# Cross-attention and routed layer on one core: first weights on ScalarE's queue, a warming of eleven products, first values loaded later

## The reference, cut to what matters

```python
# x, ctx: (8, 128, 512); 32 heads of width 128; position_bias (32, 128, 128)
h   = rmsnorm(layernorm(x)) * ln_weight
q   = h @ w_q.T;  k = ctx @ w_k.T;  v = ctx @ w_v.T          # w_q, w_k, w_v: (4096, 512)
s   = softmax(where(mask, q @ k^T + position_bias, -inf))    # per tile and head
x   = x + layernorm(x) + (s @ v) @ w_out.T
n   = layernorm(x)
r   = softmax(n @ gate_w.T)                                  # 8 experts
out = x + ((n * (r @ in_channel_scale)) @ sign(weight).T) * (r @ out_channel_scale) + bias
```

## Time and profile before

| | us |
|---|---|
| median of 3 runs | 844.12 |
| lowest and highest | 843.89, 844.49 |
| the profiled execution | 844.16 |
| its span, first to last instruction | 842.4 |
| PE busy | 833.7 (99%) |
| DVE busy | 619.5 (74%) |
| ACT busy | 392.1 (47%) |
| POOL busy | 301.4 (36%) |

### The profile page before, as it was taken

One profiled execution on the slowest core, in us unless ns is written; L12 is line 12 of the kernel. 1 busy time (PEld: TensorE's weight loads), 2 busy tenths in 40 slices (PEclk: granted clock), 3 DMA queues, 4 the chain that ended last, 5 costly groups with the idle time before them and its releaser, 6 DMA issues.

```text
span 842.4 us, 12886 instructions
## 1 busy us (share of the span) xinstructions
PE 833.7 (99%) x4356; PEld 699.5 (83%) x4356; DVE 619.5 (74%) x1005; ACT 392.1 (47%) x1009; POOL 301.4 (36%) x279
## 2 busy tenths in 40 slices
PE   9999999999999999999999999999999999999998
PEld 8878888888888878788888888888888888888886
DVE  5777856778766795877777777777777877777765
ACT  5632522432441444545544555554554455466673
POOL 2013211022030043625435444544544554535145
PEclk9999999999999999999999999999999999999999
DMA  8355463573452748423144124314413421423002
GB/s 274 138 180 184 150 237 125 168 273 117 146 192 100 224 166 267 165 100 117 51 150 154 65 96 154 102 58 157 137 50 127 153 99 63 153 92 131 1 1 101
DMA packets 60720, 114.07 MB, mean 135 GB/s; under 512 B 5208, under 2 KB 38872, under 8 KB 55408
## 3 DMA queue, kind: packets, MB, share of 16 engines
q1 hardware_dynamic: 60656, 113.25, 39.3%
HBM read 77.58 MB, written 35.65 MB: 134 GB/s over the span
## 4 chain that ended last, share of the span: by engine, by line
PE 90%; DVE 6%; issue 1%; ACT 1%; DMA 1%; POOL 1%; DVEq 0%; POOLq 0%; ACTq 0%; SPq 0%
PE out L1334 10%; PE out L1336 10%; PE out L1335 10%; PE proj L1334 9%; PE proj L1336 9%; PE proj L1335 9%; PE o L1425 6%; PE s L1406 6%; PE s L1334 3%; PE s L1335 3%; PE s L1336 3%; PE t L1414 3%; PE proj L1501 1%; PE s L1382 1%; DMA w_stage<-in_wq 1%
## 5 line engine op out<-in xcount | busy, mean ns | idle before, releaser
L926 ACT ACTIVATE probs<-probs,neg_max 128x128 f32<-128x128 f32 x256 | 99.7, 391 | 135.6 <-DVE neg_max L1179 135.6
L757 POOL TENSOR_TENSOR w_stage<-w_stage 128x256 f32<-128x256 f32 x30 | 25.2, 841 | 308.9 <-DMA w_stage<-in_wk 148.0
L769 POOL TENSOR_TENSOR w_lo<-w_stage,w_hi 128x512 fp32r<-128x512 f32 (+1 forms) x52 | 59.2, 1148 | 147.0 <-ACT w_hi L864 147.0
L1334 PE MATMUL out<-wo_hi,o_hi 128*128 128x512 f32 x224 | 95.3, 426 | 0.2 <-DVE acc L1208 0.2
L1211 DVE TENSOR_TENSOR acc<-out,acc 128x512 f32<-128x512 f32 x100 | 68.4, 688 | 35.7 <-PE out L1336 35.2
L1334 PE MATMUL proj<-x_hi,w_hi 128*128 128x512 f32 x210 | 88.5, 422 | 0.2 <-DVE ring L1038 0.2
L1336 PE MATMUL out<-wo_lo,o_hi 128*128 128x512 f32 x224 | 88.2, 394 | 0.0
L1335 PE MATMUL out<-wo_hi,o_lo 128*128 128x512 f32 x224 | 87.5, 391 | 0.0
L1336 PE MATMUL proj<-x_lo,w_hi 128*128 128x512 f32 x210 | 82.7, 394 | 0.0
L1335 PE MATMUL proj<-x_hi,w_lo 128*128 128x512 f32 x210 | 82.0, 391 | 0.0
L781 POOL TENSOR_TENSOR bias_mask<-bias_raw,mask_neg 128x512 f32<-128x512 f32 x64 | 75.7, 1194 | 13.3 <-DVE probs L1176 13.2
(11 more groups left out here) (352 smaller groups left out, 2141.9 us busy)
## 6 DMA issues: line engine op xcount, KB each, us to landing
k_spill<-ring SPq DMA_DIRECT2D x64, 256.0 KB, 2.8
v_spill<-ring SPq DMA_DIRECT2D x64, 256.0 KB, 2.2
w_stage<-in_wk SPq DMA_DIRECT2D x32, 256.0 KB, 3.3
big_stage<-in_wv SPq DMA_DIRECT2D x8, 1024.0 KB, 7.7
w_stage<-in_wq SPq DMA_DIRECT2D x32, 256.0 KB, 4.1
k_first<-k_spill SPq DMA_DIRECT2D x8, 1024.0 KB, 6.9
v_first<-v_spill SPq DMA_DIRECT2D x8, 1024.0 KB, 4.8
wo_raw<-in_wo SPq DMA_DIRECT2D x16, 512.0 KB, 3.3
```

What stands on the lines that cost most here:

```text
L769: pool.tensor_tensor(lo, staged(m, part), hi.bitcast(F32), ALU.subtract).then_inc(g_wlo, 1)
L926: last = act.activation(probs[:, j % 2, b, :], probs[:, j % 2, b, :], ACT.Exp, bias=neg_max[:, col:col + 1], accum_out=row_sum[:, col:col ...
L1334: pe.matmul(to[:], left_hi, right_hi, start=first and n == 0, stop=False, skip_group_check=True)
```

## The change

- `WARM_UP` goes from 48 to 11. The warming now multiplies a 128x128 tile of ones (in `ring`) by itself; VectorE writes the ones with a memset as its first instruction. Nothing waits for the warming's end.
- The weights of pair 0 are loaded in four halves of 128 KB (`first_load(i, k)`), of which ScalarE issues three, (0,0), (1,0) and (0,1), as its first instructions, and SP the fourth, (1,1), after the four context loads of token half 0. Each half has its own semaphore, and `plain_weights_high` waits for its half alone. The weights of pair 1 are loaded as before.
- `("XX", 3)` moves from (k+5, 4) to (k+6, 4).
- The step that loaded keys and then values is split in two, KL and VV. KL stands where it stood; the values of pair 0 move one cycle on, to (k+8, 1), behind the loads of the second pair of query weights (`w_q` pair 1, at slot 0 of that cycle). For all other pairs VV follows KL at once.

```diff
-WARM_UP = 48
+WARM_UP = 11
@@ schedule
     put(k + 5, 3, ("XT", "T4"))
-    put(k + 5, 4, ("XX", 3))
     put(k + 5, 6, ("XX", 5))
     put(k + 6, 1, ("XX", 4))
-
-    put(k + 7, 1, ("BL", 0), ("BL", 1), ("KV", 0))
+    put(k + 6, 4, ("XX", 3))
+
+    put(k + 7, 1, ("BL", 0), ("BL", 1), ("KL", 0))
+    put(k + 8, 1, ("VV", 0))
...
-    put(q + 1, 1, ("KV", 1))
+    put(q + 1, 1, ("KL", 1), ("VV", 1))
@@ loads
+        def first_load(i, k):
+
+            to, _, _ = plain_weights(0, i, k)
+            return to, wk[i][:, 2 * k:2 * k + 2].rearrange("p c d -> p (c d)")
@@ sync
-            plain_pair(0, 0)
             context(0, 0)
-            plain_pair(0, 1)
             context(0, 1)
+            to, frm = first_load(1, 1)
+            sp.dma_start(to, frm).then_inc(d_first[1][1], 16)
             context(1, 0)
             context(1, 1)
...
-            def keys_and_values(p):
+            def attention_keys(p):
                 if p >= NPAIR:
                     return
                 saved(group_at["K", p])
-                for t in range(HALF):
-                    saved(group_at["V", p // 4, t])
...
                 sp.dma_start(k_tiles[p % 2][:], k_spill[p]).then_inc(d_k[p % 2], 16)
+
+            def attention_values(p):
+                if p >= NPAIR:
+                    return
+                for t in range(HALF):
+                    saved(group_at["V", p // 4, t])
                 if p >= 2:
                     sp.wait_ge(pe_pv, last_score(p - 2))
                 sp.dma_start(v_tiles[p % 2][:], v_spill[p]).then_inc(d_v[p % 2], 16)
@@ scalar
+            for i, k in ((0, 0), (1, 0), (0, 1)):
+                to, frm = first_load(i, k)
+                act.dma_start(to, frm).then_inc(d_first[i][k], 16)
...
-                act.wait_ge(d_plain[2 * n + i], 16)
+                act.wait_ge(*((d_plain[i], 16) if n else (d_first[i][k], 16)))
@@ vector
+            dve.memset(ring[:, 0, 0, 0:P], 1.0).then_inc(v_ones, 1)
@@ tensor
             def warm_up():
-                pe.wait_ge(g_ident, 1)
+                pe.wait_ge(v_ones, 1)
                 for _ in range(WARM_UP):
-                    last = pe.transpose(s_bank[0][:, 0:P], ident[:], ident[:])
-                last.then_inc(pe_warm, 1)
-                pe.wait_ge(pe_warm, 1)
+                    pe.matmul(s_bank[0][:, 0:P], ring[:, 0, 0, 0:P], ring[:, 0, 0, 0:P], start=True, stop=True)
```

More of the change, by code:

```diff
@@ L269, in schedule @@
             steps += [("S", 4), *prod[7], *prod[3], ("T", 3), ("EXP", 4), ("BM", 5), ("BL", 4), *prod[4],
-                      *outs(0, 0), ("N", 4), ("KV", 2), *sums, ("PV", 3), *outs(0, 1, 2)]
+                      *outs(0, 0), ("N", 4), ("KL", 2), ("VV", 2), *sums, ("PV", 3), *outs(0, 1, 2)]
             continue
@@ L276, in schedule @@
         split_output = [("WO", p + 1)] if 2 * p + 2 == SPLIT else []
-        steps += slot(j + 3, prod[4] + outs(p, 0), outs(p, 1), outs(p, 2), [("KV", p + 2), *sums, *split_output])
+        steps += slot(j + 3, prod[4] + outs(p, 0), outs(p, 1), outs(p, 2), [("KL", p + 2), ("VV", p + 2), *sums, *split_output])
     j = 2 * SPLIT
@@ L436, in xattn_ffn @@
         d_w, d_big, d_ctx = [sem("d_w0"), sem("d_w1")], sem("d_big"), [sem(f"d_ctx{n}") for n in range(8)]
-        d_plain = [sem(f"d_plain{n}") for n in range(2 * PLAIN)]
+        d_plain = [sem(f"d_plain{n}") for n in range(2)]
+        d_first = [[sem(f"d_first{i}{k}") for k in range(2)] for i in range(2)]
         d_save = [sem(f"d_save{n}") for n in range(3)]
@@ L443, in xattn_ffn @@
         d_ffn_w, d_ffn_small, d_out = sem("d_ffn_w"), sem("d_ffn_small"), sem("d_out")
-        pe_warm, pe_prod, pe_x, pe_s, pe_t = [sem(n) for n in ("pe_warm", "pe_prod", "pe_x", "pe_s", "pe_t")]
+        pe_prod, pe_x, pe_s, pe_t = [sem(n) for n in ("pe_prod", "pe_x", "pe_s", "pe_t")]
         pe_pv, pe_out, pe_nt, pe_gate, pe_rt = [sem(n) for n in ("pe_pv", "pe_out", "pe_nt", "pe_gate", "pe_rt")]
@@ L461, in xattn_ffn @@
         v_y, v_ylo, v_prod, v_stats = sem("v_y"), sem("v_ylo"), sem("v_prod"), sem("v_stats")
-        v_last_res, v_n = sem("v_last_res"), sem("v_n")
+        v_last_res, v_n, v_ones = sem("v_last_res"), sem("v_n"), sem("v_ones")
         v_vsum, v_vs4, v_xsum, v_res = sem("v_vsum"), sem("v_vs4"), sem("v_xsum"), sem("v_res")
@@ L631, in plain_pair @@
             def plain_pair(m, row):
-                to = (w_stage[:, 0:3:2], w_stage[:, 5:7], w_stage[:, 1:4:2], w_stage[:, 4:8:3])[2 * m + row]
-                sp.dma_start(to, wk[2 * m + row].rearrange("p (b c) d -> p b (c d)", b=2)).then_inc(d_plain[2 * m + row], 16)
+                to = (w_stage[:, 1:4:2], w_stage[:, 4:8:3])[row]
+                sp.dma_start(to, wk[2 * m + row].rearrange("p (b c) d -> p b (c d)", b=2)).then_inc(d_plain[row], 16)
             def context(half, b):
@@ L736, in last_store @@
                 sp.dma_start(out[B - 1][:, cols], acc[:, B - 1, cols]).then_inc(d_out, 16)
-            walk({"WL": pair_weights, "DL": second_plain_pair, "VL": value_weights, "SAVE": save, "ML": mask_load, "XL": x_load, "KV": keys_and_values,
+            walk({"WL": pair_weights, "DL": second_plain_pair, "VL": value_weights, "SAVE": save, "ML": mask_load, "XL": x_load, "KL": attention_keys, "VV": attention_values,
                   "BL": bias_load, "WOL": output_weights, "AL": residual_load, "SMALL": small_loads, "FW": ffn_weights, "SUM": store, "SUML": last_store})
```

## The result

| | before | after |
|---|---|---|
| median, both timed on one chip | 844.12 (843.87 to 847.37) | 839.60 (838.66 to 839.88) |
| ratio, 95% interval | | 0.9938 (0.9919 to 0.9957) |
| span of the profiled execution | 842.4 | 837.6 |

Five executions of each. The changed kernel is faster: the medians differ by 4.5 us, the ratio says 5.2 us (3.6 to 6.8). Forecast were 3.35.

What follows compares the result with a forecast made beforehand. PE, busy 99% of the span, bounds the kernel, so only its idle or unneeded time can be won. Start 1.4, 303 us 0.55 and 329/338 us 1.4 sum to 3.35: 844.16 to 840.81 us, range 839.2 to 843.0.

Steps and rivals of the forecast that it cites:

- the landings at the start: Start: data land 0.6 us earlier, 0.4 for 128 KB less ahead and 0.2 for issue time; start gains 1.4 in all.
- The bound of 2.8 us: Start: upper bound of the gain, if the dip goes away and the weights are ready at 9.3 us.
- the dip: Start: load rate down to 180 GB/s between 5 and 6 us before the change, which another queue need not cure.
- The hand-over's terms: Keys to queries: 0.65 us at 303, 0 to 0.2 given back; 1.4 at 329 and 338, the first 0.43.
- Start, with unchanged landings: Start, k=1 group: shorter warming alone gains 0.85 us, from 12.16 to the weights' half (0,1) ready at 11.2.
- ScalarE's first piece: Start: ScalarE's first piece, at 3.79 us before; a start after 4.2 us would show the prediction wrong.
- PE's slack: Start: PE's own twelve MATMULs end at 10.0 us, 0.7 us before the k=1 group at 10.75.
- (2): Start: landings stay, as the new queue takes its share ahead of the context; start 0.85 us, 841.4; chance 0.14.
- (5): Start: ScalarE's loads go out late behind its table load, start gains 0; 842.2 to 842.7 us; chance 0.08.
- (3): Read at 338 us: set by ScalarE's table load and exponentials, not the weights; 841.8 us; chance 0.12.
- (1): Start: clock falls or rises late, 512-column MATMULs take 0.46 instead of 0.23 us; 841.8 to 843.3; chance 0.16.
- (4): Start: clock stays low through all eight products of pair 0, 11 us more, 851.8, slower than before; chance 0.05.

Runs made afterwards that it cites:

- x11: The kernel before run once more, unchanged, for a second trace: 842.86 us in one execution.
- x10: The changed kernel run once more, unchanged, against the kernel before: 838.94 us, ratio 0.9936.
- x12: Kernel before with eleven warming products of ones and first weights in whole 256 KB rows from ScalarE's queue, old hand-over: 842.73 us, ratio 0.9988.
- x4: Kernel before with only the hand-over changed (later x_lo sum of part 3, later values of pair 0), start as before: 841.78 us, ratio 0.9974.
- x6: Kernel before with only the values of pair 0 loaded later, behind the second pair of query weights: 842.12 us, ratio 0.9975.
- x2: Kernel before with only the warming changed, to eleven products of ones, all loads as before: 842.87 us, ratio 0.9993.
- x13: The changed kernel with the two altered orders of x9, and POOL's memsets and the small loads moved later: 839.75 us, ratio 0.9949 against the kernel before.
- x3: Kernel before with eleven warming products and the four weight halves, all issued from SP's one queue, old hand-over: 842.06 us, ratio 0.9974.
- x7: The changed kernel with no warming products: 841.57 us, ratio 0.9972 against the kernel before.
- x9: The changed kernel with weights' half (0,1) split before the fourth context piece and another x split two slots later: 838.84 us, ratio 0.9935 against the kernel before.
- x1: Kernel before with only the new loads (four halves, three from ScalarE's queue), old 48 transposes and hand-over: 844.37 us, ratio 1.0012.

## What the prediction had right, and the step that failed

- **The step that failed: the landings at the start.** The prediction gave earlier landings 0.6 us, 0.4 for bytes and 0.2 for the rest, "as the rate dipped to 180 GB/s between 5 and 6 us, which another queue need not cure". The context loads landed 1.5 to 1.6 us earlier (8.90 to 7.27, 9.5 to 8.0; 1.4 between x11 and x10), and the start gave 2.41 us in place of 1.4. Two things in the term were wrong. It counted at most 0.66 us of issue time as saved and took 0.2 of it, but the load that decides was issued 1.37 us sooner (3.49 to 2.12), since the second row of weights was no longer in front of it either and the loads before it were issued faster. And it held the rate fixed: from 5 to 8 us the engines moved 376 GB/s instead of 270; 3 us times the 106 GB/s between them is 318 KB, at the 318 GB/s of rows 3 one microsecond. Which of the two is the cause stays open, as said above; x12, with as many bytes ahead as before, shows that the bytes are not. The bound of 2.8 us, "if the dip goes away", held, but the dip of rows 4 was in part chance (156 to 289 GB/s there in five traces with the same loads).
- **Sign and places: right.** All the lead up to the score of unit 1 lies where the sum put it, at the start and at three MATMULs of the hand-over. The hand-over's terms came within 0.1 us each (0.66 for 0.65, 0.43 for 0.43, 1.07 for 1.0, 0.12 given back for 0 to 0.2), and x4 and x6 show each at its own place.
- **Start, with unchanged landings: right.** 0.85 was forecast, and x2 has 0.86: the weights' low part was ready at 11.21 and the group began at 11.30. That the number agrees to 0.01 is luck besides, since x2's third and fourth context loads landed within 0.02 us of those in rows 2, while in other traces with the same loads they landed up to 1.0 us sooner.
- **ScalarE's first piece: a sign that misled.** It came at 4.60, after the 4.2 that was to prove the prediction wrong, and not because of the table load, which ended at 3.43: its weights landed only at 4.6, where the weights before had landed by 3.79 (rows 2); they were now issued together with the context. It cost nothing. What mattered was the piece that ends the next group's data, not the first.
- **PE's slack: smaller than said.** "Fits with 0.7 us to spare" held for a group at 10.75. With the data at 9.7 PE's twelve MATMULs end just before (the last starts at 9.26), and in x12 PE itself is the last. More speed in the loads would now gain 0.3 us at most (9.75 against 9.26 + 0.23).
- **Rivals.** (2), landings stay, and (5), no gain at the start, fell with the trace; (3) fell with x6 (1.06 us up to 338.8). (1), the clock late, is not what happened in this execution or in x10, but it exists: of the seven traces with eleven products one (x13) shows the rise at 10.5 us, at a cost of 1.7 us of lead (2.58 to 0.86), inside the 1.0 to 2.5 us that it was priced at. (4) did not appear in any trace.
- **The total.** By the traces the parts sum to 2.41 + 0.66 + 0.43 + 1.07 less 0.34 = 4.23 us at 338.8; the end shows 4.8, the ratio 5.2 (3.6 to 6.8). The 0.5 us after 338.8 is of the size of the spread of one kernel and stays unassigned. So does part of the timed totals: x12 (1.0 us by its ratio) and x4 (2.2) together give 3.2 where the change gives 5.2 and 5.4; their leads, 2.05 at 44 us and 2.15 over the hand-over, give 4.2. The intervals are a microsecond each. From x4, which has the new hand-over, to the change the ratios give 3.0 to 3.2 us for the new start, and the traces 2.9 and 3.2 (12.67 to 9.75 and 9.49); with the old hand-over x12 gave 1.0. No run has the new hand-over with one queue, so whether a better start is worth less before the old hand-over is not shown. In their profiled executions x12 and x3, with the old hand-over, lost 0.4 and 0.9 us of lead near 349 us, but so did x7 and x9 with the new one (0.7 and 1.2); the changed kernel's two traces did not. So this is no difference between the orders that the runs could show.

## What to carry to other kernels

When a load is late, write down when it is issued, and see whether loads already issued wait while the rate is below what the same trace reaches elsewhere. Giving part of them to a second issuer changes both and is an experiment of its own, apart from moving fewer bytes. Warm PE for just as long as its data are still on their way: here none at all cost 1.9 us and twice as much cost 1.5. Put a large load behind those that something needs sooner: it was worth 1.5 us for one step moved by a cycle, and nothing waited for what was moved. And take a second trace of both kernels before a difference of half a microsecond is given a cause.

## What the runs showed of the hardware

- One issuing queue moved 249 to 287 GB/s from 5 to 8 us of this kernel, two moved 376 to 397, in fourteen traces without an exception; from 2 to 5 us there was no such difference. Why is open. From issue to landing the fourth context load took 5.2 to 6.0 us in all fourteen.
- The clock's rise moves from execution to execution, and with it the start: with 48 transposes it came between 5.2 and 7.3 us and the first needed MATMUL between 8.82 and 9.81; with eleven products it came at 4.2 to 5.3 us in six traces and at 10.5 in one; with 22 products, in one trace, at 6.1; with none at 12.0. The granted clock in the windows' rows of the start reads 1.00 throughout; only the interval of the MATMULs (0.43 or 0.23 us for 512 columns) tells.
- PE's idle stretches of up to 1.65 us between the warming and the k=1 group did not lower the clock in any trace in which it had risen. In x1's profiled execution it fell in the small work at the very end, with this row for 826 to 830 us (granted clock 0.57), and that execution lost 1.4 us there:

```profile
826.00:830.00 4.00, 4.00 (x12) 2.48 (x11) 3.07 (x8) 1.73 (x6) 1.94 (x2) 0.57 0.17 66
```

- VectorE's subtraction of two 128x512 tiles takes 0.68 us alone (298.61 in the changed kernel) and took 0.97 to 2.37 us beside POOL's instructions between 338 and 347 us (0.97 to 1.12 in the changed kernel, 2.37 and 1.95 in x3, 2.29 in x9). How much of this falls on the path changes from execution to execution (PE waited 1.41 us for it in x9, 1.09 in x3, 0.21 in the changed kernel). The Trainium skill ("GPSIMD Engine Reference", "1. Specifications") says that POOL shares its interfaces to the memory with VectorE and contends with instructions that read two tiles there; these rows agree.
